# Two-layer conditional residual block on one core: batch 1's down products of 35 of 36 tile pairs by seven block products of block sums

## The reference

```
# layer 0: mixture of experts; 8 experts and a shared one, F = 1024
g, u   = h @ Wg[e], h @ Wu[e]                    # 256 -> 1024
expert = (silu(g) * u) @ Wd[e]                   # 1024 -> 256
moe    = (1 - sg) * sum_e probs[b, e] * expert + sg * shared
x      = x + moe
# layer 1: attention over scores tanh(x W1 + b1) v, a masked softmax per position
x      = x + pooled / count
```

## Time and profile before

| | |
|---|---|
| median of 3 runs | 1131.35 us |
| profiled execution, its own time | 1131.78 us |
| its span | 1130.0 us |
| TensorE busy | 1122.1 us (99%), 4961 matmul records |
| VectorE busy | 737.8 us (65%) |
| ScalarE busy | 644.1 us (57%) |
| GpSimd busy | 297.0 us (26%), nearly all in batch 0 |
| DMA | 203.44 MB, 180 GB/s on average |

### The profile page before, as it was taken

How to read it: one execution, slowest core, us unless ns; L and a number is a source line. 1 busy time by engine, 2 the same in 40 slices (tenths; PEclk the granted TensorE clock), 3 DMA queues, 4 the chain that set the end, 5 groups by cost and what they waited for, 6 DMA issues and landing times. The chain is left out here.

```text
span 1130.0 us, 15214 instructions
## 1 busy us (share of the span) xinstructions
PE 1122.1 (99%) x4961; PEld 922.2 (82%) x4961; DVE 737.8 (65%) x1043; ACT 644.1 (57%) x1162; POOL 297.0 (26%) x350
## 2 busy tenths in 40 slices
PE   8999999999999999999999999999999999999998
PEld 6878888888888888888877788888888888888886
DVE  7997777777777777777557555555555555555556
ACT  7766656666666666666445555554545455554554
POOL 7656666444444444442003000000000000000011
PEclk9999999999999999999999999999999999999999
DMA  7655555555555655554444445444444444444402
GB/s 259 264 201 224 224 222 191 224 199 206 199 213 223 224 222 201 215 199 188 174 135 147 138 168 168 158 148 166 167 149 143 160 168 168 156 148 166 168 33 75
DMA packets 66478, 203.44 MB, mean 180 GB/s; under 512 B 6496, under 2 KB 38752, under 8 KB 66400
## 3 DMA queue, kind: packets, MB, share of 16 engines
q1 hardware_dynamic: 65584, 201.95, 49.5%
q10 hardware_dynamic: 816, 0.52, 0.1%
HBM read 115.42 MB, written 87.03 MB: 179 GB/s over the span
## 5 line engine op out<-in xcount | busy, mean ns | idle before, releaser
L1223 PE MATMUL acc_of<-h_hi,wd 128*128 128x512 f32 x576 | 225.4, 391 | 0.0
L1225 PE MATMUL acc_of<-h_lo,wd 128*128 128x512 f32 x576 | 224.2, 389 | 0.0
L1224 PE MATMUL acc_of<-h_hi,wd 128*128 128x512 f32 x576 | 224.1, 389 | 0.0
L700 ACT ACTIVATE silu<-g_ps 128x512 f32<-128x512 f32 x144 | 86.3, 599 | 222.0 <-PE g_ps L1225 222.0
L987 DVE SCALAR_TENSOR_TENSOR v_both<-silu,gates,v_both 128x512 f32<-128x512 f32 x144 | 108.7, 755 | 142.9 <-PE v_both L1225 142.5
L694 ACT ACTIVATE v_both<-g_ps 128x512 f32<-128x512 f32 x144 | 83.8, 582 | 196.5 <-PE g_ps L1225 195.0
L967 DVE TENSOR_TENSOR gate<-e_ps,v_part 128x512 f32<-128x512 f32 x144 | 99.4, 690 | 119.2 <-PE e_ps L1225 119.1
L1223 PE MATMUL v_both<-xs_hi,wq 128*128 128x512 f32 x432 | 168.8, 391 | 1.3 <-DVE up L972 0.9
L1225 PE MATMUL v_both<-xs_lo,wq 128*128 128x512 f32 x432 | 168.2, 389 | 0.0
L1224 PE MATMUL v_both<-xs_hi,wq 128*128 128x512 f32 x432 | 168.1, 389 | 0.0
L631 POOL MEMSET x<- 128x16 f32 x2 | 0.2, 114 | 504.5 <-PE v_both L1225 504.5
(11 more groups left out here) (199 smaller groups left out, 1845.8 us busy)
## 6 DMA issues: line engine op xcount, KB each, us to landing
wq_kept<-wq SPq DMA_DIRECT2D x72, 896.0 KB, 4.8
wq<-wq_kept SPq DMA_DIRECT2D x72, 896.0 KB, 4.5
wd_kept<-wd SPq DMA_DIRECT2D x36, 512.0 KB, 6.3
wd<-wd_kept SPq DMA_DIRECT2D x36, 512.0 KB, 3.3
raw_d<-in_L_cond_Wd SPq DMA_DIRECT2D x32, 256.0 KB, 5.5
raw<-in_L_cond_Wg SPq DMA_DIRECT2D x31, 256.0 KB, 2.6
raw<-in_L_cond_Wu SPq DMA_DIRECT2D x31, 256.0 KB, 3.2
out_x<-x SPq DMA_DIRECT2D x8, 256.0 KB, 2.1
```

The source lines that it names most:

```text
L700: nc.scalar.activation(silu0[:, i % 2, :], g_ps[:], ACT.Silu).then_inc(silu0_done, 1)
L1223: nc.tensor.matmul(ps, w_hi, a_hi, start=start, stop=False, skip_group_check=True)
L1224: nc.tensor.matmul(ps, w_lo, a_hi, start=False, stop=False, skip_group_check=True)
L1225: return nc.tensor.matmul(ps, w_hi, a_lo, start=False, stop=stop, skip_group_check=True)
```

## The change

**Batch 1's down products.** With h of a pair as blocks a11 (half 0, even tile), a12 (half 0, odd tile), a21 (half 1, even), a22 (half 1, odd), the 8 products of a pair become 7, of a11, a12, a22 and four sums s1 to s4, with weight blocks of which four are sums as well (ABOUT gives the weight block of each). This is done for pairs p = 0 to 34 of batch 1 (SPS = 35); pair 35 keeps its eight products, in `last_pair`. Batch 0 is multiplied as before.

```diff
+        ABOUT = {"a11": 0, "a12": 2, "s4": 3, "s1": 4, "s3": 5, "s2": 6, "a22": 7}
+        P_BANK = {"a11": acc[0][0][:], "s3": acc[1][0][:], "s2": acc[0][1][:]}
+        TURN = acc[1][1][:]
+        TURNS = ("a22", "a12", "s1", "s4")
+        def turn_of(i):
+            r = i - NU
+            q = TURNS[r % 4]
+            k = r // 2 - 2
+            return q, [p for p in (k, k + 1) if 0 <= p < SPS]
```

Three products (a11, s3, s2) accumulate over all pairs in a bank each. The other four take turns in the fourth bank, two pairs at a time (`turn_sum`), and after each turn VectorE adds the bank to a quarter of `xT` (`empty`). TensorE's slot:

```diff
                 first_bank(L1_STEP.get(i))
-                if i >= LAG:
+                if i >= NU + LAG:
+                    p = (i - NU) // PAIR - 1
+                    if i % PAIR == 0:
+                        own_sum("a11", p)
+                        own_sum("s3", p)
+                    else:
+                        own_sum("s2", p)
+                elif i >= LAG:
                     down(0, i - LAG)
...
+                if i >= NU + LAG:
+                    turn_sum(i)
+                elif i >= LAG:
                     down(1, i - LAG)
-            for t in range(NT):
-                down(t, NG - LAG)
-            for t in range(NT):
-                down(t, NG - 1)
+            last_pair()
```

**The sums of h** are made by GpSimd during batch 1, four 128 x 512 operations a pair:

```diff
+            def sums_h(p):
+                i = NU + p * PAIR
+                pool.wait_ge(h_done[1], i + 1)
+                pool.wait_ge(h_done[0], i + 1)
+                if p:
+                    pool.wait_ge(c_split["s2"], p)
+                    pool.wait_ge(sum_made["s4"], p)
+                nc.gpsimd.tensor_tensor(s3[:], a_own[:], a21[p % 2][:], ALU.subtract).then_inc(sum_made["s3"], 1)
+                pool.wait_ge(sum_made["s3"], p + 1)
+                pool.wait_ge(h_done[1], i + 2)
+                nc.gpsimd.tensor_tensor(a21[p % 2][:], a21[p % 2][:], a_own[:], ALU.add).then_inc(sum_made["s1"], 1)
+                pool.wait_ge(c_split["s3"], p + 1)
+                nc.gpsimd.tensor_tensor(s3[:], a_own[:], s3[:], ALU.subtract).then_inc(sum_made["s2"], 1)
+                pool.wait_ge(sum_made["s2"], p + 1)
+                pool.wait_ge(h_done[0], i + 2)
+                pool.wait_ge(c_split["a12"], p + 1)
+                nc.gpsimd.tensor_tensor(a12[:], a12[:], s3[:], ALU.subtract).then_inc(sum_made["s4"], 1)
```

h of batch 1 is now written to SBUF. ScalarE rounds each of the seven (`round_c`), VectorE makes each rest (`rest_c`), in a new order written out by hand for even and odd slots (here VectorE's):

```diff
+            def even(i, p):
+                second_gate(i)
+                if i == L1_AT:
+                    add_acc(1, end_of_b[0])
+                empty(i - 1)
+                second_up(i)
+                hidden_second(i)
+                second_layer_bank(L1_STEP.get(i))
...
+                    rest_c("s1", p - 1)
+                    rest_c("s2", p - 1)
+                hidden_first(i)
+                if p:
+                    rest_c("s4", p - 1)
...
+                rest_c("a11", p)
+                second_layer(L1_STEP.get(i))
+            def odd(i, p):
+                second_gate(i)
+                empty(i - 1)
+                second_up(i)
+                hidden_second(i)
...
+                    rest_c("s3", p)
...
+                hidden_first(i)
...
+                rest_c("a22", p)
+                rest_c("a12", p)
```

**The sums of the down weights** are made by GpSimd in batch 0, into four more blocks of `wd`, so that stores and fetches of `wd` grow from 512 KB to 1 MB:

```diff
+            def sums_d(k):
+                w = raw_d[:, k % RAWS]
+                td_made(nc.gpsimd.tensor_tensor(w[:, 4:6, :], w[:, 1:4:2, :], w[:, 0:2, :], ALU.subtract))
+                td_made(nc.gpsimd.tensor_tensor(w[:, 6, :], w[:, 3, :], w[:, 4, :], ALU.subtract))
+                td_made(nc.gpsimd.tensor_tensor(w[:, 7, :], w[:, 2, :], w[:, 6, :], ALU.subtract))
+                hi, lo = wd[:, k % DR, 0, 4:DN, :], wd[:, k % DR, 1, 4:DN, :]
+                nc.gpsimd.tensor_tensor(hi, w[:, 4:DN, :], zero[:, 0:1].unsqueeze(2).broadcast_to([P, DN - 4, P]),
+                                        ALU.add).then_inc(td_hi_done, 1)
+                pool.wait_ge(td_hi_done, k + 1)
+                nc.gpsimd.tensor_tensor(lo, w[:, 4:DN, :], hi.bitcast(F32), ALU.subtract).then_inc(td_split, 1)
...
+                if n == 3:
+                    sums_d(0)
+                if n % PAIR and n > 1:
+                    sums_d(n // PAIR)
```

and SP waits for them:

```diff
                 if n % PAIR == PAIR - 1:
                     k = n // PAIR
-                    sp.wait_ge(d_split, n + 1)
+                    sp.wait_ge(td_split, k + 1)
                     if m < NU // PAIR:
                         load_d(sp, m)
                     sp.dma_start(wd_kept[k], wd[:, k % DR].bitcast(F32)).then_inc(wd_stored[k % DR], 16)
```

**The end of batch 1.** The bank of a11 is copied by ScalarE to `res` and added to a quarter of `xT`; then `res` takes up the banks of s2 and, after `hidden_first(143)` and two of GpSimd's four `join` additions, of s3 (`res_step` 1 to 3). `last_pair` waits for `res_step` 3:

```diff
+                for f in range(PAIR):
+                    for t in range(NT):
+                        q = (("a11", "s3"), ("a12", "a22"))[f][t]
+                        if f == 0:
+                            pe.wait_ge(res_step, (3, 2)[t])
+                            down_sum(("a12", "a22")[t], SPS - 1, acc[0][t][:], True, False)
+                            if t:
+                                pe.wait_ge(emptied, LAST_TURN - FIRST_TURN + 1)
+                        pe.wait_ge(c_split[q], SPS + 1)
+                        for d in range(KD):
+                            w = f * KD + d
+                            mm = three_pass(acc[d][t][:], wd[:, k % DR, 0, w], wd[:, k % DR, 1, w], *home(q, SPS),
+                                            f == 0 and d == 1, f == 1)
```

More of the change, by code:

```diff
@@ L46, in cond_resid_kernel @@
     DR = 3
+    DN = 8
     RAWS = 2
@@ L200, in cond_resid_kernel @@
             at += S * 4
-            e_diag.append(place(f"e_diag{b}", [P, NJ, P], F32 if b else F32R, at))
+            e_diag.append(place(f"e_diag{b}", [P, NJ, P], F32, at))
             at += S * 4
@@ L447, in _ @@
                 sp.dma_start(wq[:, i % WR].bitcast(F32), wq_kept[n]).then_inc(wq_fetched[i % WR], 16)
[L448 to L451, removed]
+                if n % PAIR == 0 and n:
+                    fetch_d(n // PAIR - 1)
+            fetch_d(SPS)
             for b in range(B):
@@ new lines, in join, with joined_to @@
+            def join():
+                joins = [0]
+                def joined_to(d, t, src):
+                    dst = xT[:, 1, d, t * BANK:(t + 1) * BANK]
+                    joins[0] += 1
+                    nc.gpsimd.tensor_tensor(dst, dst, src, ALU.add).then_inc(joined, 1)
+                    pool.wait_ge(joined, joins[0])
+                pool.wait_ge(emptied, LAST_TURN - FIRST_TURN)
+                joined_to(1, 0, xT[:, 1, 1, BANK:2 * BANK])
+                pool.wait_ge(res_step, 2)
+                joined_to(1, 0, res[:])
+                pool.wait_ge(res_step, 3)
+                joined_to(0, 1, res[:])
+                joined_to(1, 1, res[:])
@@ L633, in _ @@
                 if b == 0:
-                    split_x1()
+                    for p in range(SPS):
+                        sums_h(p)
+                    join()
             pool.wait_ge(p_done[3], NG)
             pool.wait_ge(x1_ones, B)
-            pool.wait_ge(x1_split, NB)
             pool.wait_ge(diag_zeroed, B)
@@ L864, in _ @@
                     round_x(1, q)
+            def even(i, p):
+                if p:
+                    round_c("s1", p - 1)
+                    round_c("s2", p - 1)
+                seed(i + 1)
+                gate_second(i)
+                first_bank(L1_STEP.get(i))
+                if p:
+                    round_c("s4", p - 1)
+                gate_first(i + 1)
+                if p == SPS:
+                    round_c("s3", p)
+                keep_p7(i + 1)
+                round_c("a11", p)
+                keep_v(i + 1)
+                second_bank(L1_STEP.get(i))
+            def odd(i, p):
+                if p < SPS:
+                    round_c("s3", p)
+                if i + 1 < NG:
+                    seed(i + 1)
+                gate_second(i)
+                if p == SPS:
+                    act.wait_ge(c_used["a11"], SPS)
+                    nc.scalar.activation(res[:], P_BANK["a11"], ACT.Copy).then_inc(p1_kept, 1)
+                if i + 1 < NG:
+                    gate_first(i + 1)
+                round_c("a22", p)
+                if i + 1 < NG:
+                    keep_p7(i + 1)
+                round_c("a12", p)
+                if i + 1 < NG:
+                    keep_v(i + 1)
+            for p in range(SPS + 1):
+                even(NU + p * PAIR, p)
+                odd(NU + p * PAIR + 1, p)
             exp_blocks(0)
@@ L1154, in second_layer_bank @@
                     prob_args(0, k - 6)
-            for i in range(NG):
+            for i in range(NU):
                 second_gate(i)
@@ new lines, in last_pair @@
+            def last_pair():
+                k, done = SP0 + SPS, {}
+                pe.wait_ge(wd_fetched[k % DR], (SPS // DR + 1) * 16)
+                for f in range(PAIR):
+                    for t in range(NT):
+                        q = (("a11", "s3"), ("a12", "a22"))[f][t]
[9 more added lines that the diff above has]
+                                            f == 0 and d == 1, f == 1)
+                        mm.then_inc(down_done[t], 1)
```

356 lines of the change are left out of this document (233 added, 123 removed).

## The result

The changed kernel takes **1128.65 us** (median of 10 runs, 1127.42 to 1129.60) against 1131.48 for the kernel before in the same comparison: ratio 0.9973, interval 0.9965 to 0.9981. It is faster, by 2.8 us; the forecast was 1123, 8.4 us faster. The profiled execution took 1127.99 us, span 1126.1.

The account below looks back on a forecast made before the run. TensorE's count of matmuls was taken as the bound in both batches. Terms -23.8 + 0.5 + 7.75 + 1 + 1.8 + 3.05 + 1.5 = -8.2 on 1131.78, less 0.43, gave 1123 us; range 1112 to 1133.

Parts of the forecast that it names:

- rival (a): Start of batch 0: no stall there, everything else as forecast; 1112.5 us, chance 0.13.
- Part 1: Batch 1's down products: 35 pairs use 7 products in place of 8, -23.8 us if nothing else stalls TensorE.
- Part 2: Batch 1: VectorE with GpSimd needs about 13.5 us per pair against TensorE's 14.28, so it keeps up: 0 us.
- (b): Batch 1: VectorE with GpSimd becomes the bound, product 3 waiting in odd slots; 1143 us, slower, chance 0.12.
- (c): Batch 1: partial stalls of about 0.25 us per pair, 8.5 us; 1131.5 us, no change, chance 0.1.
- product 3 waiting for `up1`: Odd slots of batch 1: the place where VectorE would first hold TensorE up, with 0.47 us of slack.
- The term of +0.5: Batch 0's second-layer steps put up to 1.4 us of VectorE work into one even slot, half covered: +0.5 us.
- Part 3: Start of batch 0: GpSimd's weight sums delay SP, ScalarE, then TensorE at slot 3: +7.75, later +1, clock +1.8 us.
- The lower clock: Behind the stall at slot 3: 8 matmuls at 1.2 GHz, each dearer by 0.2267 us: +1.8 us.
- Part 4: The end: last slot's `up1` late, +0.8, and last_pair waiting, +2.25, together +3.05 us; block sums in F32 +1.5.

Follow-up runs that it names:

- e4: The changed kernel without GpSimd's sums of down weights (their places zeroed once) and with SP waiting for `d_split` again; 1113.10 us.
- e9: The changed kernel with two extra unread 128x512 GpSimd operations ahead of its third sum, in 34 pairs of batch 1; 1164.95 us.
- e6: The changed kernel with one extra unread 128x512 GpSimd operation behind its fourth sum, in 34 pairs of batch 1; 1126.94 us.
- e1: The changed kernel with only SP's order changed: d sums' wait, down-weight load and store issued one use later; 1125.88 us.
- e3: The changed kernel with GpSimd's constants, flags and two mask sets moved from uses 13, 17, 21, 25 to 21, 33, 43, 55; 1126.08 us.
- e7: The changed kernel with the edits of e2, e3 and e5 together; 1114.59 us.
- e5: The changed kernel with VectorE's end reordered: third product sum earlier without waiting for GpSimd's join, last emptyings moved; 1125.06 us.
- e2: The changed kernel with GpSimd's sums of down weights one pair later and SP's wait, load and store deferred too; 1118.91 us.
- e8: The changed kernel with one extra unread 128x512 GpSimd operation ahead of its third sum, in 34 pairs of batch 1; 1130.43 us.

## Why the prediction was wrong, step by step

The direction was right (0.76 on faster), and so was the mechanism of most terms; the size was not: 1123 against 1128.65, 8.4 us of gain against 2.8. By the table, from slot 72 to the end of the span the kernel gains 18.7 us (14.77 + 3.9). The forecast's terms for that part were -23.8 + 0.5 + 3.05 + 1.5 = -18.75, and e4, which has no loss in batch 0, takes 1113.10 where rival (a) had 1112.5. The error is in batch 0: 14.8 us lost where 10.55 were forecast. That is 4.2 us, of which 0.8 lie at the start, 2.7 at the second step and 0.7 in the creep behind it; another 1.1 come from profiled executions against medians (I took 0.43 off, while the profiled execution of after lies 0.66 below its median), 0.1 from what lies outside the span.

- **Part 1** held: 105 matmuls fewer, 0.68 us less per pair from slot 96 on, no hole in the middle of batch 1.
- **Part 2** held in its result, 0 us: rivals (b) and (c) are refuted for this kernel, since TensorE has no wait in the middle of batch 1. Where the next limit lies the forecast did not see. It gave ScalarE 8.5 of 14.28 us and no wait, and named product 3 waiting for `up1`; in e9 it is gate_end that waits, for `seed` behind the rounding of s2, in a loop over three engines that has room for one more operation of GpSimd. For the exclusion of two-input VectorE operations and GpSimd, which the Trainium skill states (SBUF — State Buffer, Who interferes with whom), see the rest at 811.02: 1.27 us beside GpSimd against 0.68 alone. The same section frees VectorE operations with at most one SBUF input from it; e6 agrees: its extra operation (805.50, 1.04 us) runs beside the up sum (805.34), which takes 0.69 us as without it. The term of +0.5 for the steps of batch 0's second layer is not to be seen: from slot 72 to 96 the kernel gains 9.1 us, where by the code 39 matmuls are gone, 8.8 us. That the terms of this part meet the measured 18.7 so closely is in part luck.
- **Part 3, the stall at slot 3**: 7.75 forecast, 7.94 measured (46.70 - 38.53 less one matmul's 0.23), by the links named up to `seed`. The lower clock held for 12 matmuls, not 8: 12 x 0.2 = 2.4 us against 1.8. With about 1 us of waits for `up1` behind it, 11.35 against 10.55. Rival (a), no stall, is refuted. But the link named was not the only one: with the store of use 2 ahead of SP's wait (e1) some 5 of the 11.35 us go, and 6.4 stay, by way of `load_gu(3)` and the combine of pair 3. The forecast lists that load behind the wait and does not follow it.
- **The step that failed** is the sentence in Part 3: "In the steady part GpSimd idles 7.45 us per pair before its next combine, which covers it." The idle time was read at one place and spent on the d sums, 5.5 us a pair. But GpSimd's list also holds constants, flags and two sets of masks at uses 13, 17, 21 and 25, and one set of masks takes 9.3 us. With the d sums a pair without these pieces takes GpSimd 12.4 us (198.74 less 186.34, the combine before), so it catches up 2.6 us per pair where a set of masks puts it back by 7.0 (22.0 - 14.96). It worked without a gap from 46.81 to 312.84, its lead was used up at the fourth piece, and TensorE paid 2.7 us at slot 27 (1.4 to 5.3 in the other traces with this batch 0). e3 moves the four pieces and nothing else, and this step is gone.
- A creep of 0.7 us from slot 30 to 72 was not forecast either; it is gone without the d sums (e4) and 0.3 us in e7. I did not look for its place.
- **Part 4** held: the two holes are 0.78 + 2.52 us beyond a matmul's step (3.05 forecast), and e5 bears out what the second waited for: `hidden_first(143)` and the join, ahead of the third product sum. The block sums of batch 0 with the transposes among them take 3.78 us (1103.20 to 1106.98) where they took 2.19 (1108.78 to 1110.97): 1.59 against 1.5.

Timeline of TensorE after, block sums:

```profile
1103.20 1.12 PE L1654 MATMUL v_both<-x,e_diag 128*128 128x258 f32 x4
...
1104.27 2.78 PE L1654 MATMUL v_both<-x,e_diag 128*128 128x258 f32 x12
1106.98 0.38 PE L1614 MATMUL acc_of<-blk_max_diag,ones 8*128 8x8 f32 x2
```

## What to carry to other kernels

Before work is put on an idle engine, add up its whole list over the stretch with the least room, one-off pieces included: the idle time of a quiet pair covers the new work only where nothing else stands. Where a queue in order gets a new wait, look at what stands behind it: here 14.8 of 18.7 us gained were lost again to GpSimd's sums and the wait for them, and letting both trail by one pair, with the masks moved apart, brought 11.8 of them back (14.77 - 2.97) without removing any work. And a loop's margin is better measured than composed, by an operation added in the chain and one beside it; the wait that grows then tells where the limit is, and here it was not where it had been composed.

## What the hardware showed that was not expected

- After the wait of 7.8 us at slot 3, twelve matmuls ran at 1.2 GHz. After the wait of 2.4 us ahead of last_pair the executions differ: in the profiles of e1, e2, e3 and e8 the next seven to eight matmuls start 0.43 us apart (granted clock 0.91 from 1080 to 1100 in e1), which costs some 1.6 us, while in those of after, e4, e6 and e9 they keep to 0.23 after the same wait.
- The same operation in the same place of GpSimd's list took 0.60 us in one execution and 1.32 in another (the second `mask_part` of masks(1), at 206.75 in the profile of e6 and at 207.09 in that of after). Where GpSimd's list is full the loss of batch 0 varies too: 12.9 to 15.6 us at slot 72 in five traces with the same batch 0. The runs of after spread over 2.2 us and those of e8 over 4.2, against 0.6 for e7, in which GpSimd has gaps. That such small differences are what spreads them is my inference; the stretches at the lower clock above are another source.
